# A feed-forward stage's three products: two levelled half-precision parts a side in place of two fp32r parts

## What is computed

```python
def fp4_quant_dequant(x):                 # blocks of 16 along the last dim
    scale = jnp.maximum(jnp.max(jnp.abs(xb), axis=-1, keepdims=True) / 6.0, 1e-12)
    idx = jnp.searchsorted(_MID, jnp.abs(xb / scale))
    q = _GRID[idx] * jnp.sign(xn) * scale
def fp4_linear(x, w):
    return jnp.einsum('bsk,nk->bsn', fp4_quant_dequant(x), fp4_quant_dequant(w))
...
mod = (_silu(L0_c) @ L0_wmod).reshape(B, 6, 1, -1)     # sa, ca, ga, sb, cb, gb
h = _layernorm(x) * (1 + ca) + sa
x = x + ga * attention(h)
h = _layernorm(x) * (1 + cb) + sb
gate, y = fp4_linear(h, w_gate), fp4_linear(h, w_up)
x = x + gb * fp4_linear(_silu(gate) * y, w_down)
```

## Time and profile before

| | |
|---|---|
| median of three runs | 1687.57 us (1687.49 to 1687.82) |
| the profiled execution's own time | 1687.39 us |
| its span in the profile | 1686.1 us |
| busy in the span: PE, DVE, ACT, POOL | 1639.9, 1580.5, 1374.2, 777.2 us |
| granted TensorE clock, mean | 0.998 |

### The profile page before, as it was taken

One profiled execution on the slowest core, in us unless ns is written; L12 is line 12 of the kernel. 1 busy time (PEld: TensorE's weight loads), 2 busy tenths in 40 slices (PEclk: granted clock), 3 DMA queues, 4 the chain that ended last, 5 costly groups with the idle time before them and its releaser, 6 DMA issues.

```text
span 1686.1 us, 38834 instructions
## 1 busy us (share of the span) xinstructions
PE 1639.9 (97%) x15446; PEld 814.2 (48%) x15446; DVE 1580.5 (94%) x1708; ACT 1374.2 (82%) x2508; POOL 777.2 (46%) x1625
## 2 busy tenths in 40 slices
PE   8999999999999999999999999999999999999998
PEld 7743233333333333673333333333333379999997
DVE  7899999999999999769999999999999879988887
ACT  5499999999999999669999999999999833333332
POOL 3034445454444445303444544566654457555542
PEclk9999999999999999999999999999999999999999
DMA  6102111112111112511111121111112533534420
GB/s 233 64 8 71 52 50 45 45 45 71 51 51 52 46 45 76 163 43 44 46 46 45 45 69 51 51 52 46 46 45 63 157 114 126 155 125 152 148 67 19
DMA packets 83103, 123.15 MB, mean 73 GB/s; under 512 B 4706, under 2 KB 69098, under 8 KB 82922
## 3 DMA queue, kind: packets, MB, share of 16 engines
q1 hardware_dynamic: 82506, 120.15, 22.4%
q10 hardware_dynamic: 416, 0.53, 0.1%
HBM read 74.52 MB, written 46.15 MB: 72 GB/s over the span
## 4 chain that ended last, share of the span: by engine, by line
DVE 63%; PE 32%; ACT 2%; issue 2%; POOL 1%; DMA 0%; ACTq 0%; POOLq 0%; DVEq 0%
DVE nm L1073 60%; PE acc L443 13%; PE slot L443 10%; PE acc L610 6%; PE slot L666 1%; PE slot L581 1%; DVE ost L1086 1%; ACT e_sb L820 1%; PE slot L464 0%; DMA v_sb<-in_wmod 0%; PE acc L641 0%; DVE qs L1140 0%; DVE e_sb L1128 0%; ACT e_sb L749 0%; DVE e_sb L1147 0%
## 5 line engine op out<-in xcount | busy, mean ns | idle before, releaser
L1073 DVE TENSOR_REDUCE nm<-slot 128x1 f32<-128x1024 f32 x1024 | 1166.1, 1213 | 20.6 <-PE slot L581 18.5
L820 ACT ACTIVATE e_sb<-slot,nm 128x1024 f32<-128x1024 f32 x1024 | 1136.9, 1112 | 17.5 <-DVE nm L1073 12.6
L610 PE MATMUL acc<-e_sb,vp 64*64 64x512 f32 x8192 | 1060.9, 594 | 6.3 <-DVE ost L1086 4.7
L581 PE MATMUL slot<-stq,stk 64*64 64x512 f16 x4096 | 411.5, 388 | 21.6 <-ACT e_sb L820 21.6
L581 PEld LDWEIGHTS slot<-stq,stk 64*64 64x64 f16 x4096 | 117.6, 103 | 625.8 <-ACT e_sb L820 592.1
L610 PEld LDWEIGHTS acc<-e_sb,vp 64*64 64x64 f32 x8192 | 283.3, 132 | 188.6 <-issue 74.0
L1308 POOL TENSOR_TENSOR dlt<-nm 128x4 f32<-128x4 f32 x128 | 25.6, 200 | 412.1 <-DVE nm L1073 412.1
L820 ACT ACTIVATION_READ_ACCUMULATOR e_sb<-slot,nm 128x1 f32 x1024 | 199.8, 195 | 0.0
L1299 POOL TENSOR_TENSOR vp<-v_sb,fac 128x512 f32<-128x512 f32 x128 | 133.4, 1042 | 10.2 <-POOL fac L1289 0.3
L1285 POOL TENSOR_TENSOR rtot<-tot,mone 128x4 f32<-128x4 f32 x128 | 132.7, 1037 | 10.0
L1279 POOL TENSOR_TENSOR wsum<-cor,ssum 128x8 f32<-128x8 f32 x128 | 25.9, 202 | 234.2 <-ACT cor L850 234.2
(11 more groups left out here) (179 smaller groups left out, 1926.8 us busy)
## 6 DMA issues: line engine op xcount, KB each, us to landing
o_r<-o_heads SPq DMA_DIRECT2D x32, 1024.0 KB, 7.5
stk<-qk_parts SPq DMA_DIRECT2D x128, 128.0 KB
o_heads<-ost_hi SPq DMA_DIRECT2D x64, 256.0 KB, 3.4
o_heads<-ost SPq DMA_DIRECT2D x64, 256.0 KB, 4.1
v_sb<-in_x SPq DMA_DIRECT2D x16, 512.0 KB, 6.5
qk_parts<-e_sb SPq DMA_DIRECT2D x32, 256.0 KB, 2.4
stq<-qk_parts SPq DMA_DIRECT2D x128, 64.0 KB
out<-e_sb SPq DMA_DIRECT2D x32, 128.0 KB, 1.8
```

What stands on the lines that cost most here:

```text
L581: mm = pe.matmul(slot[s][side * VD:(side + 1) * VD, c * 512:(c + 1) * 512], stk[c * 64:c * 64 + 64, h % 2, i * P + side * VD:i * P + (side ...
L610: mm = pe.matmul(acc[half * VD:(half + 1) * VD, c * 512:(c + 1) * 512], vp[rows, g % 3, gi, half, :], e_v[rows, j % ERING, n0:n0 + 512], s ...
L820: act.activation(e_v[:, j % ERING, half * 1024:(half + 1) * 1024], slot[u % 3][:, :], ACT.Exp, bias=nm[:, g % 4, i, half:half + 1], accum_ ...
L1073: dve.tensor_reduce(nm[:, g % 4, i, half:half + 1], slot[u % 3][:, :], AX.X, ALU.max, negate=True).then_inc(maxed.sem)
```

## The change

Every product of the feed-forward stage takes float16 parts. So that they lie well in that format's range, the weights, the input and the folded down weights are multiplied by powers of two (`lift`) before they are split, and the results by the inverse (`undo`). The powers come from maxima: DVE reduces the block maxima of the weights to one number a partition (`tops`); SP sends these 128 x 2 numbers to DRAM (`weight_tops`) and loads them back to every partition (`all_tops`, 128 x 256); a new function `levels`, called by DVE at the end of the preparation of b = 1, reduces these and the modulation rows and makes `lift` and `undo`. The hidden tile has a level of its own for each token: it is put into the scales (`qs`) by DVE in `mix_snap`, and its inverse (`h_undo`) is made by POOL in `scale_mix` and applied in `finish`.

```diff
@@ sync_program
                     sp.dma_start(rows_d.rearrange("v b d -> b v d"), mrow[0:B, :, :]).then_inc(rows_out.sem, 16)
+                sp.wait_ge(*top_made.past(2 * b + 1))
+                sp.dma_start(tops_d[b], tops[:, 2 * b:2 * b + 2]).then_inc(tops_out.sem, 16)
+                if b:
+                    sp.wait_ge(*tops_read.past(b - 1))
+                sp.wait_ge(*tops_out.past(b))
+                sp.dma_start(all_tops[:, :].rearrange("p (q n) -> p q n", n=2),
+                             tops_d[b:b + 1].to_broadcast([P, P, 2])).then_inc(got_tops.sem, 16)
                 for j in range(JT + LAG):
@@ parts (placed as F16 in the same regions; gate and up high parts too)
-        xqT_lo = place("xqT_lo", [P, 2, 2, P], E_AT + 6368 * 4, F32R)
-        xqT_hi = place("xqT_hi", [P, 2, 2, P], WQ_AT, F32R)
+        xqT_lo = place("xqT_lo", [P, 2, 2 * P], E_AT + 6368 * 4, F16)
+        xqT_hi = place("xqT_hi", [P, 2, 2 * P], WQ_AT, F16)
@@ take_x, silu (ACT)
-            high(xqT_hi[:, i % 2].rearrange("p a b -> p (a b)"), acc[:, 768:1024]).then_inc(xq_high.sem)
+            b = i // NT
+            act.activation(xqT_hi[:, i % 2, :], acc[:, 768:1024], ACT.Copy, scale=lift[:, 1 + b:2 + b]).then_inc(xq_high.sem)
@@ weight_step
             elif s == 2:
+                dve.tensor_reduce(tops[:, 2 * b + part:2 * b + part + 1], amax, AX.X, ALU.max).then_inc(top_made.sem)
                 ins = dve.reciprocal(inv, scale)
@@ prepare_dve
                 weight_step(b, s)
+            if b:
+                levels()
+
+        def levels():
+            top = wide_max[:, 3, 0:1]
+            dve.wait_ge(*got_rows.past(0))
+            for n, rows in enumerate((cb1, sbr, gb)):
+                dve.tensor_reduce(wide_max[:, n, :], rows[:, :, :], AX.X, ALU.max, apply_absolute_value=True)
+            dve.wait_ge(*got_tops.past(0))
+            dve.tensor_reduce(peak[:, 0:1], all_tops[:, :], AX.X, ALU.max).then_inc(tops_read.sem)
+            dve.wait_ge(*tops_read.past(0))
+            dve.scalar_tensor_tensor(peak[:, 1:3], wide_max[:, 0, :], float(D) ** 0.5, wide_max[:, 1, :], ALU.mult, ALU.add)
+            dve.wait_ge(*got_tops.past(1))
+            settle(dve.tensor_reduce(top, all_tops[:, :], AX.X, ALU.max))
+            settle(dve.tensor_scalar(peak[:, 3:5], wide_max[:, 2, :], top, None, ALU.mult))
+            settle(dve.tensor_scalar(peak[:, :], peak[:, :], LEAST, None, ALU.max))
+            settle(dve.tensor_scalar(size[:, :].bitcast(I32), peak[:, :].bitcast(I32), EXPONENT, None, ALU.bitwise_and))
+            settle(dve.reciprocal(lift[:, :], size[:, :]))
+            settle(dve.tensor_scalar(lift[:, :], lift[:, :], 2.0 ** 14, None, ALU.mult))
+            settle(dve.tensor_scalar(undo[:, :], size[:, :], 2.0 ** -14, None, ALU.mult))
+            dve.tensor_scalar(undo_gu[:, :], undo[:, 1:3], undo[:, 0:1], None, ALU.mult).then_inc(levels_made.sem)
+            dve.wait_ge(*levels_made.past(0))
@@ mix_normalise, mix_snap
             settle(dve.tensor_scalar(scale, amax, 1.0 / 6.0, 1e-12, ALU.mult, ALU.max))
+            if lo == 0:
+                dve.tensor_reduce(h_top[:, i % 4:i % 4 + 1], qs[:, 1, 0:44], AX.X, ALU.max)
             settle(dve.reciprocal(inv, scale))
+            if lo == 0:
+                top = h_top[:, i % 4:i % 4 + 1].bitcast(I32)
+                dve.tensor_scalar(h_lift[:, i % 4:i % 4 + 1].bitcast(I32), top, EXPONENT, EXPONENT,
+                                  ALU.bitwise_xor, ALU.bitwise_and)
+                dve.tensor_scalar(h_size[:, i % 4:i % 4 + 1].bitcast(I32), top, EXPONENT, None, ALU.bitwise_and)
...
             dve.wait_ge(*mix_added.past(i - 1))
+            if lo == 0:
+                dve.tensor_scalar(qs[:, 1, 0:44], qs[:, 1, 0:44], h_lift[:, i % 4:i % 4 + 1], 2.0 ** 11, ALU.mult, ALU.mult)
@@ low_x, finish (low_h stays a plain subtraction, hidden_product takes undo_gu in the same way)
-            low(dve, xqT_lo[:, i % 2].rearrange("p a b -> p (a b)"), acc[:, 768:1024],
-                xqT_hi[:, i % 2].rearrange("p a b -> p (a b)")).then_inc(xq_low.sem)
+            dve.scalar_tensor_tensor(xqT_lo[:, i % 2, :], acc[:, 768:1024], lift[:, 1 + b:2 + b], xqT_hi[:, i % 2, :],
+                                     ALU.mult, ALU.subtract).then_inc(xq_low.sem)
-            dve.tensor_tensor(outb[:, i % 3, :], x2_r[:, i % 7, :], down_at(i), ALU.add).then_inc(out_made.sem)
+            dve.scalar_tensor_tensor(outb[:, i % 3, :], down_at(i), h_undo[:, (i + 3) % 4:(i + 3) % 4 + 1], x2_r[:, i % 7, :],
+                                     ALU.mult, ALU.add).then_inc(out_made.sem)
@@ scale_mix (POOL)
             if lo == 0:
+                b = (i - 3) // NT
+                pool.tensor_scalar(h_undo[:, i % 4:i % 4 + 1], h_size[:, i % 4:i % 4 + 1], undo[:, 3 + b:4 + b], 2.0 ** -12,
+                                   ALU.mult, ALU.mult)
                 pool.tensor_tensor(blocks(mix_q[:, i % 2, 0:F]), blocks(mix_n[:, 0:F]), wide(qs[:, 1, 0:44], 44),
                                    ALU.mult).then_inc(hid_scaled.sem)
```

More of the change, by code:

```diff
@@ L152, in adaln_block @@
         qs = sb("qs", [P, 3, 88])
+        tops = sb("tops", [P, 2 * B])
+        all_tops = sb("all_tops", [P, 2 * P])
+        peak = sb("peak", [P, 5])
+        size = sb("size", [P, 5])
+        lift = sb("lift", [P, 5])
+        undo = sb("undo", [P, 5])
+        undo_gu = sb("undo_gu", [P, B])
+        wide_max = sb("wide_max", [P, 4, B])
+        h_top = sb("h_top", [P, 4])
+        h_lift = sb("h_lift", [P, 4])
+        h_size = sb("h_size", [P, 4])
+        h_undo = sb("h_undo", [P, 4])
         constants = sb("constants", [P, 2])
@@ L228, in adaln_block @@
         outb = region(e_sb, 10080, 3, D)
-        xqT_lo = place("xqT_lo", [P, 2, 2, P], E_AT + 6368 * 4, F32R)
-        xqT_hi = place("xqT_hi", [P, 2, 2, P], WQ_AT, F32R)
-        hqT_lo = place("hqT_lo", [P, 2, FCH, P], E_AT + 8544 * 4, F32R)
-        hqT_hi = [upper[:, 4:7, 512 + s * D:512 + (s + 1) * D] for s in range(2)]
+        xqT_lo = place("xqT_lo", [P, 2, 2 * P], E_AT + 6368 * 4, F16)
+        xqT_hi = place("xqT_hi", [P, 2, 2 * P], WQ_AT, F16)
+        hqT_lo = place("hqT_lo", [P, 2, FCH * P], E_AT + 8544 * 4, F16)
+        hqT_hi = place("hqT_hi", [P, 2, FCH * P], E_AT + 8544 * 4 + 3072, F16)
         gu = [slot[0], slot[1]]
@@ L654, in down @@
                 pe.wait_ge(*out_made.past(i - 1))
-            products(down_at(i), [(hqT_lo[:, i % 2, c, :], hqT_hi[i % 2][:, c // 2, c % 2 * P:(c % 2 + 1) * P], wdb_lo[b][:, c, :],
-                                            wdb_hi[b][:, c, :]) for c in range(FCH)]).then_inc(down_mm.sem)
+            products(down_at(i), [(hqT_lo[:, i % 2, c * P:(c + 1) * P], hqT_hi[:, i % 2, c * P:(c + 1) * P], wdb_lo[b][:, c, :],
+                                   wdb_hi[b][:, c, :]) for c in range(FCH)]).then_inc(down_mm.sem)
         def turn_h(i):
@@ L680, in gate_up @@
                     mm = products(gu[w][:, c * 512:c * 512 + 352],
[L681 to L682 removed]
+                                  [(xqT_lo[:, i % 2, k * P:(k + 1) * P], xqT_hi[:, i % 2, k * P:(k + 1) * P],
+                                    wgu_lo[k][:, n0:n0 + 352], wgu_hi[k][:, n0:n0 + 352]) for k in range(2)])
                 mm.then_inc((up_mm if w else gate_mm).sem)
```

40 lines of the change are left out of this document (23 added, 17 removed).

## The result

The changed kernel took 1714.24 us (median of six runs, 1713.86 to 1720.66), the kernel before 1687.53 beside it: 1.0171 times as long, 95% interval 1.016 to 1.0182. The prediction was 1704, with 1710 as the end of its range: the sign was right, 10 us are missing. The profiled execution has a span of 1712.5 us.

What follows compares the result with a forecast made beforehand. The prediction took DVE's maxima to bound attention (PE its first seven steps) and PE alone the tiles after it. 1687.4 + 16.7 (wait) + 1.7 (clock) - 2 (tiles) = 1703.8, called 1704 us; 8-in-10 range 1696 to 1710.

Steps and rivals of the forecast that it cites:

- Term 1, the wait: In levels, before the attention of b = 1: DVE waits for the maxima's trip to DRAM and back, about +16.7 us.
- gb as a twin: Earlier transfer issued behind stack transfers, landing 13.1 us later as two engines ran dry; taken to show the maxima's delay.
- the backlog: Stack transfers queued on two DMA engines until about 752.6; the maxima were to reach DRAM only behind them, at 753.2.
- Term 2, the clock: Attention of b = 1, behind PE's stand of some 16 us: a lower granted clock costs about +1.7 us.
- Term 3, the tiles: Tiles after attention: 9.7 us each instead of 9.75, about -2 us in all, ends -6 and +4.
- the loop over POOL takes PE's place: In the tiles: the loop DVE, POOL, DVE becomes the bound instead of PE, at 9.7 us a tile.
- POOL's small instruction, put at 0.14: In the tiles' loop over POOL: the one small instruction added to POOL's part costs 0.14 us a tile.
- The loop before, put at 9.07: Tiles before the change: the loop over DVE and POOL itself takes 9.07 us, from 9.22 less a 0.15 us stand.
- DVE's part of the loop, put at 0.5: Tiles, DVE's part behind L1145: four small instructions add 0.4 us and scalar operands perhaps 0.1.
- The start and the three last tiles, put at 0: Ends of the tile stage: faster matmuls give back 0.3 us each, small instructions lose 0.3 each.
- tiles at PE's pace: Rival for the tiles: POOL's and DVE's additions overlap, a tile takes 9.3 us, total 1693.8; chance 0.09.
- The rival of dear small instructions: Rival for the tiles: small instructions cost 0.2 us each, the loop takes 10.1 us, total 1715; chance 0.1.

Runs made afterwards that it cites:

- the queue of ACT: The changed kernel with ACT issuing both weight_tops and all_tops of b = 1 on its own queue, SP sending only the stacks: 1695.62 us.
- pe_warm_longer: The changed kernel with 170 idle turns on PE ahead of the scores of step 1 of b = 1, the wait kept: 1713.34 us.
- levels_late: The changed kernel with the second half of levels moved behind the last maximum of b = 1: 1695.91 us, 1.0051 of the kernel before.
- undo_last: The changed kernel with POOL making h_undo at the end of its iteration instead of ahead of the 704-wide product: 1702.61 us.
- bare_tile: The changed kernel without the level of each hidden row (three instructions of mix_normalise, one of mix_snap, POOL's h_undo left out): 1697.94 us.

## Why the prediction was right and where it was wrong

- **Term 1, the wait (16.7).** Right in mechanism and place. Foreseen: issue 742.5, landing 753.2, load back 2.5, first maximum 757.6. Measured: 740.49, 751.9, 2.9, 756.96, in an execution that was 1.8 us ahead; with that added, 742.3, 753.8, 2.9 and 758.8. The agreement to 0.6 us at the first maximum was luck: the landing came 0.6 later than foreseen, the load back took 0.4 more, and the term is 18.6 between the first maxima where it had 17.4 (16.7 with 0.7 taken off for PE's slack; that 0.7 no run shows by itself). What it said of gb as a twin held; that the backlog delays the transfer is supported by the queue of ACT.
- **Term 2, the clock (1.7).** Measured 1.8 by pe_warm_longer's stretch. Both together: 18.3 by the medians of levels_late, 20.4 to 20.7 by the traces, foreseen 18.4.
- **Term 3, the tiles (-2, ends -6 and +4).** This is the step that failed: +7.8 by the traces, +8.3 by levels_late. The 9.8 us between -2 and +7.8 are nearly all of the miss (1713.9 against 1703.8 in the profiled executions); terms 1 and 2 were 2.0 short, and the lead of 1.8 hid that. The mechanism (the loop over POOL takes PE's place) held; its sizes did not. Of the 9.8, 6.3 lie in tiles 3 to 28 (foreseen -1.4, measured +4.9), 2.9 in the start and the end (foreseen 0), 0.6 in the rounding to -2.
  - *POOL's small instruction, put at 0.14.* The row it came from the earlier trace rows shows the distance of two small instructions of another kind, tensor by tensor. This one, with two scalar factors, takes 0.27, has 0.10 ahead of it and 0.06 behind, and costs the 256-wide product ahead of it its overlap with the next: L1429 to L1435 is 1.05 us, where L1365 to L1368 was 0.58 (1519.13 to 1519.71). The difference, 0.47, is three times the term. undo_last shows what it decided: with it away this loop is no longer the bound, and the period is 9.43.
  - *The loop before, put at 9.07.* Start to start it is 8.91: 1.24 from L1156 to L1365, 0.58 to L1368, 1.52 to L1145, 4.41 to L1153 where DVE doesn't wait, 1.16 to L1156. The 0.15 us taken off the 9.22 for the stand ahead of L1117 was too little, for two instructions that don't wait overlap: L1117 starts 0.33 us after L1173 in the iteration ahead (1515.39 and 1515.72), and 0.56 in that one (1524.38 and 1524.94). This error was to the other side and made good half of the one on POOL's instruction.
  - *DVE's part of the loop, put at 0.5.* It measured 0.50: 0.39 for the four small instructions (0.4 foreseen), 0.06 each because the instructions behind L1224 and L1235 start that much later (0.1 foreseen for scalars), and 0.01 less for the rest. L1180, 0.06 longer too, lies outside the loop. 8.91 + 0.47 + 0.50 = 9.88, the period measured.
  - *The period taken as one number for 27 tiles.* Tiles 3 to 9 took 10.33 us, 3.1 us in all. The prediction had read L1147 in late tiles only; in the early ones it took 1.41 us already before instead of 1.16, beside POOL's folds, and PE, being the bound, hid that. With the loop over POOL as the bound it showed, and L1207 took 1.61: 9.88 + 0.46 is the 10.33 measured. A stretch in which an engine has extra work is a stage of its own.
  - The start and the three last tiles, put at 0, lost 1.2 and 1.7. In the last ones DVE's and POOL's additions lie bare on the chain, more than the matmuls give back (24 in 3.77 us there instead of 4.12). The 1.2 at the start go with the place of POOL's small instruction: in undo_last, which has it at the end of the iteration, tiles 0 to 3 take 0.04 us less than before the change.
- **What PE gains.** The spacing fell from 161 to 150 ns at 352 columns and from 118 to 109 at 256; bare_tile's period of 9.31 is the 9.30 that the prediction worked out from the gap of N/2.4 + 2.5 ns in the Trainium skill, TensorE: Matmul & The Clock Gate, section on the back-to-back issue gap (149 and 109 ns). That rival (tiles at PE's pace) failed on the loop, not on the matmul.
- **The rival of dear small instructions** (loop at 10.1, time 1715, chance 0.1) came nearest in time, and for a related reason: not all five were dear, POOL's was, and the early tiles and the ends cost what it had put on the rest.
